# Fourteen identity products on TensorE between the last transposes of the self-attention and the values of its last half

## The reference

```python
x = x + xattn(layernorm(x), ctx)            # softmax(x ctx^T) ctx, 4096 context rows
x = x + attn(layernorm(x), w_attn, w_proj)  # 16 heads of 16, bias slope*rel, causal

def attn(x):
    q, k, v = split(x @ w_attn.T)
    att = softmax(q k^T / sqrt(D) + where(rel <= 0, slope * rel, -inf))
    return (att @ v) @ w_proj.T

x = x + ffn(layernorm(x))                   # top 32 tokens of each of 8 experts
```

## Time and profile before

| | us |
|---|---|
| three executions | 122.81, 124.24, 124.9 |
| their median | 124.24 |
| the profiled execution, device time | 122.81 |
| its span | 121.1 |
| TensorE busy in the span | 108.1 |
| VectorE busy in the span | 77.5 |

### The profile page before, as it was taken

The page is one execution under the profiler, slowest core; times in us unless marked ns, Lnnn a source line. Parts: engine busy times, 40 slices in busy tenths (PEclk is TensorE's granted clock), DMA queues, the critical chain, the costliest instruction groups (busy, mean ns, idle before and its releaser), DMA issues.

```text
span 121.1 us, 2466 instructions
## 1 busy us (share of the span) xinstructions
PE 108.1 (89%) x958; PEld 89.0 (73%) x958; DVE 77.5 (64%) x194; ACT 60.3 (50%) x114; POOL 50.6 (42%) x65
## 2 busy tenths in 40 slices
PE   4999999999999999999998959892987995899981
PEld 4968888888999999999978648681955794334540
DVE  0699889977659697357339799979044797021212
ACT  4377779549869657541248894870011302514100
POOL 2499999999999999911010000010001400300000
PEclk9999999999999999999999999999599999999999
DMA  2995999995999400006989898000000000000002
GB/s 98 375 405 166 401 355 353 419 424 219 346 433 433 179 5 0 0 5 173 520 346 520 346 514 346 11 8 0 5 0 0 0 0 0 5 0 0 0 5 87
DMA packets 3756, 22.72 MB, mean 188 GB/s; under 512 B 544, under 2 KB 800, under 8 KB 3232
## 3 DMA queue, kind: packets, MB, share of 16 engines
q1 hardware_dynamic: 3744, 22.55, 47.1%
HBM read 22.29 MB, written 0.26 MB: 186 GB/s over the span
## 4 chain that ended last, share of the span: by engine, by line
PE 78%; DVE 15%; issue 3%; ACT 1%; POOL 1%; POOLq 0%
PE bank L842 6%; PE bank L844 6%; PE bank L843 6%; PE bank L816 6%; PE bank L820 6%; PE bank L823 6%; PE bank L935 6%; PE bank L1028 6%; PE bank L832 6%; PE bank L798 3%; PE bank L904 3%; PE bank L1043 3%; PE bank L882 3%; DVE att_T L562 3%; PE bank L916 2%
## 5 line engine op out<-in xcount | busy, mean ns | idle before, releaser
L360 POOL TENSOR_TENSOR rstd<-vareps,power 128x1 f32<-128x1 f32 x6 | 3.3, 553 | 41.7 <-DVE vareps L450 41.6
L399 POOL TENSOR_SCALAR bias<-rel 128x384 f32<-128x384 f32 x16 | 20.0, 1254 | 1.1
L842 PE MATMUL bank<-v_hi,p_hi 128*128 128x258 f32 x64 | 19.4, 303 | 0.0
L844 PE MATMUL bank<-v_hi,p_lo 128*128 128x258 f32 x64 | 18.0, 282 | 0.0
L843 PE MATMUL bank<-v_lo,p_hi 128*128 128x256 f32 x64 | 18.0, 281 | 0.0
L498 DVE TENSOR_TENSOR p_lo<-bank,p_hi 128x512 fp32r<-128x512 f32 x16 | 10.9, 686 | 7.9 <-ACT p_hi L680 7.9
L680 ACT ACTIVATE p_hi<-bank 128x512 fp32r<-128x512 f32 x16 | 9.6, 598 | 8.1 <-PE bank L832 8.1
L798 PE MATMUL bank<-ident 128*128 128x128 f32 x74 | 11.5, 319 | 1.7 <-POOL ident L354 1.6
L798 PEld LDWEIGHTS bank<-ident 128*128 128x128 f32 x74 | 10.7, 225 | 2.3 <-POOL ident L354 1.6
L726 ACT ACTIVATE att<-att,nmax 128x128 f32<-128x128 f32 (+1 forms) x32 | 11.9, 444 | 0.8 <-DVE nmax L554 0.8
L843 PEld LDWEIGHTS bank<-v_lo,p_hi 128*128 128x128 f32 x64 | 12.2, 190 | 0.0
(11 more groups left out here) (120 smaller groups left out, 198.6 us busy)
## 6 DMA issues: line engine op xcount, KB each, us to landing
k_in<-ctx_t SPq DMA_DIRECT2D x8, 512.0 KB, 4.6
v_in<-ctx_v SPq DMA_DIRECT2D x8, 512.0 KB, 6.3
wdn_sb<-w_down SPq DMA_DIRECT2D x2, 2048.0 KB, 9.5
wup_hi<-w_up SPq DMA_DIRECT2D x1, 4096.0 KB, 11.9
wup_lo<-w_up SPq DMA_DIRECT2D x1, 4096.0 KB, 18.4
wqkv_sb<-w_qkv SPq DMA_DIRECT2D x1, 768.0 KB, 10.9
x_sb<-x_in SPq DMA_DIRECT2D x1, 256.0 KB, 2.7
wproj_sb<-w_proj SPq DMA_DIRECT2D x1, 256.0 KB, 11.0
```

What stands on the lines that cost most here:

```text
L399: nc.gpsimd.tensor_scalar(bias[:, h], rel[:, :], SLOPES[h], None, ALU.mult).then_inc(bias_ready, 1)
L842: nc.tensor.matmul(hi, p_hi[:, h % PB, n], v_hi[:, i, n], start=(i == 0 and n == 0), stop=False)
L844: last = nc.tensor.matmul(hi, p_lo[:, h % PB, n], v_hi[:, i, n], start=False, stop=(i == NCH - 1 and n == NT - 1))
```

## The change

One constant and one call are new. Fourteen products of the identity with itself go into bank 0, behind the transposes of units 9 to 11 and ahead of the waits for the copies of units 8 to 11. Bank 0 held scores of the self-attention, which VectorE has read by then, and is written next by the router. No wait, no transfer and no other engine's list changes.

```diff
+WARM_BEFORE_HEADS = 14
@@
             values_of_heads(0, 1)
             for n in range(9, NU):
                 transpose_unit(n)
+            keep_warm(banks[0], WARM_BEFORE_HEADS)
             for n in range(8, NU):
                 wait_copied(pe, n)
```

## The result

| | before | changed |
|---|---|---|
| executions | 122.47, 122.81, 124.24, 124.9 | 123.16, 124.07, 124.1, 124.37 |
| median | 123.53 | 124.08 |
| profiled execution | 122.81, span 121.1 | 124.1, span 122.4 |
| mean granted clock of the profiled one | 0.986 | 0.986 |

Ratio of changed to before: 1.0146, 95% interval 1.0079 to 1.0213. By this ratio the change made the kernel slower by about 1.5%, and the interval excludes no change. The forecast was a small gain. The times in the table show less: the medians are 0.55 us apart (0.4%), the means 123.61 and 123.93 us (0.3%). So the size of the loss is not settled by this comparison.

What follows compares the result with a forecast made beforehand. It took the kernel to be bound by a chain through the last half's values, slowed by a clock fall after idle TensorE. 1.51 us won less 0.89 overfill gave 0.62, hence 123.6 us at the middle execution, range 121.9 to 125.0.

Steps and rivals of the forecast that it cites:

- the local sum: From the last transposes to the end of the last half's values: 1.51 us won less 0.89 lost, gain 0.62 us.
- overfill: Ahead of the last half's values: the products need 3.35 us in a gap of 2.46, delaying the values by 0.89 us.
- the same 0.62 from each of the three: Whole kernel: the profiled execution's gain of 0.62 us taken off all three earlier times, the middle one giving 123.6 us.
- the fall in the gap: Between the last transposes and the last half's values: TensorE's clock drops to half at 84.74 us, for 3.4 us.
- the term of 1.51 us: Last half's values: they cost 3.40 us at the slow clock and 1.89 at full clock, so 1.51 us is won.
- the rival: Gap ahead of the values: without a clock fall that hits the values, products are pure delay, 0.89 us slower; chance 0.2.
- The slow stretch moves on: Behind the router, at the experts' first product: the clock falls there instead, 0.9 us slower in all, 125.1; chance 0.13.
- The products don't hold the clock: Gap ahead of the values: the clock falls at 84.74 all the same, 0.95 us slower, 125.2 at median level; chance 0.07.
- the products cost half: Gap ahead of the values: fourteen products fit in 1.6 us, so the whole 1.51 us is won; chance 0.03.
- three of its rivals: Pure delay in the gap (125.1 us, chance 0.2), clock not held (125.2, 0.07), slow stretch moved behind the router (125.1, 0.13).

Runs made afterwards that it cites:

- the later place filled: Three products behind each of the two small transposes behind the router, none in the gap, against the kernel before: mean 122.64 us, ratio 1.0056.
- the first comparison: The changed kernel with fourteen products against the kernel before, the runs of the result table: median 124.08 us, ratio 1.0146.
- the run of twenty-eight: Twenty-eight products in place of fourteen ahead of the waits, against the kernel before: mean device time 126.02 us, ratio 1.0343, four executions.
- the second: The changed kernel run again without edit, twelve executions against 35 of the kernel before: mean 122.83 beside 122.80 us, ratio 1.005.

## Why the prediction went wrong

**Right: the local sum.** Price of the products 0.112 us an instruction; overfill 0.89 (executions at full clock: 0.90); values 1.89 at full clock (1.88); net 0.62 in an execution whose clock had fallen there (0.62 to 0.64 in the profile). The copies were as long as before, 0.68 to 0.69. The spacing at the low clock, 0.213, was read from the kernel's first products, where the granted clock's row shows 1.00; the run with the products behind the waits bears it out, with 15 starts between 85.76 and 88.96 us under a clock of 0.50.

**Wrong: "the same 0.62 from each of the three".** This is the step that failed. The kernel before was read from one execution, and the fall in the gap was taken as a property of the kernel: the term of 1.51 us was given to every execution, with a frequency of one. It is a property of the execution. Over all comparisons the 75 executions of before are 30 with no fall, 35 with one, 10 with two: 0.73 falls each, at both places together. A fall costs 1.3 to 1.7 us (121.16 - 119.83 between the means of before; 1.51 and 1.69 in the two profiles). In the 30 executions without one the products can only cost, and they cost the whole 0.89; so the products also lift the best time, 119.4 to 120.3 in span. The prediction had the balance in hand: it said that loss and gain cancel at 0.59 falls in the gap an execution. But it turned the share round: it wrote that the rival decides if the gap costs no clock in more than about six of ten executions, where its own 0.59 gives more than about four of ten. It gave that rival 0.2 and the gain 0.5, with nothing but one profile to tell the frequency. How many of before's 0.73 falls lie in the gap is bounded only: 8 of 12 executions fell with the later place filled (0.67), and with the gap filled by seven, ten or fourteen, 12 of 36 still fell (0.33; with the first comparison and the run of twenty-eight 15 of 44), which leaves 0.4. By these, 0.89 - 1.5 x 0.67 = -0.1 and 0.89 - 1.5 x 0.4 = +0.3 us: about nothing, to slightly slower. The second split fits the kernel before by itself: two places that fall independently, in 0.4 and 0.33 of the executions, would give 10 of 75 with two falls and 30 with none, which are the counts (though 8 of the 10 came in one comparison).

**The sign against the sum.** In the first comparison three of four executions of the changed kernel fell; in the second three of twelve did. With so few executions and steps of 1.5 us, the median moves by which group it lands in. The 1.5% of the first comparison may be that in part; the second gives 0.5%, with an interval that just holds no change, and a difference of the means of 0.02 +- 0.34 us. The forecast gain of 0.62 lies outside the intervals of both ratios and about two standard errors from the difference of the means. What is shown clear of noise is the 0.90 +- 0.13 us that the products cost at full clock; that they lose 1.5% overall is not shown.

**"The slow stretch moves on"** had 0.13 and describes the profiled execution, down to the place behind the router; its price was given as 1.5, and it is 1.69. As a cause it was wrong: a prevented fall doesn't come later in its place, since 9 of 12 executions of the changed kernel had no fall and none of 36 had one with both places filled. That the fall behind the router happens without the products too is inferred, as no profile of before shows one there: 10 of 75 executions of before have two falls, and none of 12 had two once that place was filled.

**"The products don't hold the clock"** and **"the products cost half"** are out: in every profiled execution with work in the gap the values ran at full clock, and 28 instructions took 3.1 us.

The range, 121.9 to 125.0, held the median, 124.08; it was drawn from the spread of before and not from the effect, so that it held says nothing for the sum. The times that it gave three of its rivals, 125.1 and 125.2, lay outside it.

The Trainium skill, page "TensorE: Matmul & The Clock Gate", section "What's actually happening", says of the clock's rise at the start of a kernel that its moment is not tied to that start, so that the count of slow matmuls varies from run to run. The counts here show such a variation for falls in the middle of a kernel: 30, 35 and 10 of 75 executions with none, one and two. The prediction cited the remark and then summed as if one execution stood for all.

## What to carry to other kernels

A loss that one profile shows in the clock is a loss of that execution; before it is bought off with work on the path, count over many executions how often it occurs, and multiply. Filling work must end before the wait that it fills does: here ten products hid wholly, and fourteen cost 0.9 us. Work that hides costs little, so it is worth trying in every quiet place ahead of dense work at once: here filling one of the two won up to 0.7 us in the mean, filling both won 1.3 and took the spread away. Where times come in groups, compare the groups and their shares, not one median of four.

## What the runs showed of the hardware

The clock fell in the wake of a wait of 2.19 us, but only in an estimated 0.4 to 0.67 of the executions by the bounds above, and then at moments that differ against the same work: at 84.74 ahead of the values, and in other runs at 85.64 and 85.96, within the work behind the wait. In the profile of the changed kernel it fell behind the router, where no single wait was over 0.7 us but TensorE was busy for 2.24 of 3.80 us. In all four profiles with a fall the clock stayed low for 3.4 us, in one of them with TensorE busy throughout (3.00 of 3.00 us).

Executions at full clock still spread by about 1 us in span with the same kernel (before: 119.4 to 120.7). Part of it lies in the cross-attention: in three profiles, one of them of the changed kernel, two of VectorE's subtractions for k_lo in a row took 1.76 and 2.05 us (the group's mean is 1.4 in the kernel before), TensorE waited for the second near 24 us, and the last transposes came 0.5 to 0.7 us later than in the changed kernel's first profile (82.89, 82.97 and 83.09 beside 82.37). Another profile, of seven products with the later filling, was as late (82.90) without this wait, so it is not the only source. The second of them in the changed kernel, and the products that waited:

```profile
22.60 2.05 DVE L476 TENSOR_TENSOR k_lo<-k_in,k_hi 128x1024 fp32r<-128x1024 f32 x1
...
24.71 0.73 PE L824 MATMUL bank<-k_lo,q_hi 128*128 128x512 f32 x2 [0.41 <-DVE k_lo L476]
```

GpSimd worked on v_lo for part of the time of both (20.96 to 22.58 and from 23.65 us on); whether that slows the subtraction was not tried.
